# Routing the first half of the tokens earlier in a fused attention and mixture-of-experts kernel

## The reference

```python
x = L0_attn_x
h = _layernorm(x, axis=-1) * (1 + ca) + sa
x = x + ga * _L0_attn_ref(h, WQ, WK, WV, WO)      # causal attention, 16 heads of 8 channels
h = _layernorm(x, axis=-1) * (1 + cb) + sb
x = x + gb * _L0_ffn_ref(h, ...)                  # shared expert + routed experts

# _L0_ffn_ref: E = 64 experts in 8 groups; 4 groups kept, K = 6 experts for each token
shared = silu(x @ sg_w.T) * (x @ su_w.T) @ sd_w.T
scores = sigmoid(x @ gate_w.T) + gate_bias
...                                               # keep the best 4 groups, then the best 6 scores
comb = weights of the 6 chosen experts, normalised
h = silu(einsum('th,eih->eti', x, eg_w)) * einsum('th,eih->eti', x, eu_w)
routed = einsum('eti,ehi,te->th', h, ed_w, comb)
```

## Time and profile before

| | us |
|---|---|
| median of 3 runs | 1053.04 |
| lowest and highest | 1044.67, 1057.72 |
| the profiled execution, device time | 1046.67 |
| its span, first to last instruction | 1045.0 |
| PE busy in it | 869.2 |
| DVE busy | 724.9 |
| ACT busy | 565.3 |
| POOL busy | 253.7 |
| mean granted clock of TensorE, share of full | 0.912 |

### The profile page before, as it was taken

One profiled execution on the slowest core, in us unless ns is written; L12 is line 12 of the kernel. 1 busy time (PEld: TensorE's weight loads), 2 busy tenths in 40 slices (PEclk: granted clock), 3 DMA queues, 4 the chain that ended last, 5 costly groups with the idle time before them and its releaser, 6 DMA issues. The chain is left out here.

```text
span 1045.0 us, 13432 instructions
## 1 busy us (share of the span) xinstructions
PE 869.2 (83%) x4333; PEld 448.6 (43%) x4333; DVE 724.9 (69%) x1323; ACT 565.3 (54%) x888; POOL 253.7 (24%) x348
## 2 busy tenths in 40 slices
PE   6899999999885439998996006789999999998998
PEld 3553443444222219887886002333433443343433
DVE  4879888888476616655663234679988988997575
ACT  4324666666762105554553003649768877875743
POOL 1011222222115777714751771000000000000000
PEclk9899999999986579999998557879999999998999
DMA  3732565542012126746772112000000010000001
GB/s 88 236 79 45 190 198 172 160 144 70 23 53 93 51 87 216 229 158 200 225 222 92 52 51 73 0 0 9 2 23 11 7 46 1 0 1 0 1 0 41
DMA packets 51054, 87.48 MB, mean 84 GB/s; under 512 B 11202, under 2 KB 22832, under 8 KB 49200
## 3 DMA queue, kind: packets, MB, share of 16 engines
q1 hardware_dynamic: 36716, 58.56, 18.8%
q10 hardware_dynamic: 8128, 15.47, 4.0%
q0 software_dynamic: 6144, 12.60, 3.9%
HBM read 43.28 MB, written 40.89 MB: 81 GB/s over the span
## 5 line engine op out<-in xcount | busy, mean ns | idle before, releaser
L1066 ACT ACTIVATE pt<-psum 128x1024 f32<-128x1024 f32 (+1 forms) x192 | 149.9, 814 | 111.5 <-PE psum L808 111.1
L1218 DVE TENSOR_REDUCE part_max<-psum 128x1 f32<-128x512 f32 (+3 forms) x304 | 184.3, 658 | 31.6 <-PE psum L790 19.1
L786 PE MATMUL psum<-ka,qa 72*128 72x512 bf16 (+3 forms) x384 | 113.7, 337 | 5.4 <-DVE part_max L1218 2.0
L746 POOL DMA_INDIRECT part<-slot_y,slot_row x96 | 92.9, 968 | 86.5 <-DMA slot_y<-pt 57.8
L735 POOL DMA_INDIRECT slot_x<-va,slot_row x96 | 96.3, 1004 | 36.4 <-issue 29.0
L725 POOL TENSOR_SCALAR_AFFINE_SELECT pt<-pt 128x256 f32<-128x256 f32 x128 | 52.3, 410 | 215.4 <-ACT pt L1066 214.8
L808 PE MATMUL psum<-qa,ka 75*128 75x512 bf16 (+3 forms) x384 | 94.5, 328 | 3.0 <-ACT pt L1066 1.4
L824 PE MATMUL psum<-pt,va_g 128*32 128x512 f32 (+3 forms) x768 | 82.7, 503 | 0.5 <-POOL pt L725 0.3
L1426 DVE TENSOR_TENSOR moe_hid<-moe_silu,psum 128x256 f32<-128x256 f32 x56 | 23.4, 418 | 84.6 <-ACT moe_silu L1186 78.8
L110 ACT ACTIVATE ln_sq<-psum 128x512 f32<-128x512 f32 x44 | 26.1, 594 | 98.4 <-PE psum L93 98.3
L786 PEld LDWEIGHTS psum<-ka,qa 72*128 72x128 bf16 x384 | 37.1, 98 | 79.4 <-DVE part_max L1218 60.0
(11 more groups left out here) (316 smaller groups left out, 1650.3 us busy)
## 6 DMA issues: line engine op xcount, KB each, us to landing
slot_x<-zero ACTq DMA_DIRECT2D x8, 1792.0 KB, 7.0
pt<-slot_x SPq DMA_DIRECT2D x56, 256.0 KB, 3.4
slot_y<-pt SPq DMA_DIRECT2D x56, 256.0 KB, 2.0
qa<-in_moe_gu SPq DMA_DIRECT2D x4, 1024.0 KB, 6.3
qa<-rows_q SPq DMA_DIRECT2D x21, 192.0 KB
ka<-rows_k SPq DMA_DIRECT2D x21, 192.0 KB
wt_c<-in_channel_w SPq DMA_DIRECT2D x4, 576.0 KB, 4.2
o_den<-acc SPq DMA_DIRECT2D x32, 64.0 KB, 2.1
```

What stands on the lines that cost most here:

```text
L746: pool.indirect_dma_start(out=yg[:, n % 4, j, :], out_offset=None, in_=ys_d[b], in_offset=bass.IndirectOffsetOnAxis(ap=row[:, n, j:j + 1], ...
L786: mm = pe.matmul(bank[:, nk * h:nk * (h + 1)], qa[0:ROWS, g % RING, h0 + h, chunk(i, P)], ka[0:ROWS, g % RING, h0 + h, k0:k0 + nk], start= ...
L1066: act.activation(pt[:, u % 4, :, 0:n], score_bank[u % 2][:, :, 0:n], ACT.Exp, scale=SCALE)\
L1218: dve.tensor_reduce(part_max[:, h0:h0 + heads, slot], bank_of("fill", f)[:, 0:heads * nk].rearrange("p (h n) -> p h n", h=heads), AX_X, AL ...
```

## The change

The whole routing of batch 0 moves from group 7 and behind it into groups 3 to 6. A table, `STEP_AT`, gives each step of pieces 0 and 1 a unit, counted from EARLY = 72, the first unit of group 3; each step takes a place in the rotation of the three banks 4, 5 and 7 instead of a bank of its own, so the item three places on waits for its reader. DVE's and ACT's parts stand at the same units or a few later. `positions` is cut in parts (`counts`, `ranks`; `tile_ends`, `slot_keys`, `slot_rows`). For pieces 0 and 1 ACT copies the centred values to `G.h`, so that their bank comes free before `modulated` reads them. Scatters of batch 0 are issued one for each unit of `SCATTER_AT`: units 158 to 167 and 176 to 183, 18 in all; the other 30 follow the last mask. Behind attention, PE and DVE start with piece 2 at once.

```diff
+    EARLY = NU * 3
+    STEP_AT = {("project", 0): EARLY + 18, ("centre", 0): EARLY + 22, ("variance", 0): EARLY + 26, ("logits", 0): EARLY + 31,
+               ("turn_h", 0): EARLY + 34, ("project", 1): EARLY + 50, ("centre", 1): EARLY + 54, ("variance", 1): EARLY + 58,
+               ("logits", 1): EARLY + 63, ("turn_h", 1): EARLY + 66, ("count", 0): EARLY + 81, ("rank", 0): EARLY + 82,
+               ("experts", 0): EARLY + 88}
...
-        ITEMS += [("fill", f) for f in BACK[unit]]
+        ITEMS += [("fill", f) for f in BACK[unit]] + [item for item, at in STEP_AT.items() if at == unit]
+    SCATTER_AT = [u for u in range(EARLY + 86, NU * NG) if u < NU * LAST or 8 <= u - NU * LAST < 16]
...
+            if was == "project":
+                pe.wait_ge(x_new, k + 1)
+            if was == "centre":
+                pe.wait_ge(ln.squared, n0 + k + 1)
+                pe.wait_ge(centre_kept, k + 1)
...
-        centre_bank = [G.bank[4], G.bank[7], G.bank[4], G.bank[6]]
+        centre_bank = [bank_of("centre", 0), bank_of("centre", 1), G.bank[4], G.bank[6]]
...
+                        if NU * g + u in SCATTER_AT:
+                            scatter(0, SCATTER_AT.index(NU * g + u))
+                for k in range(len(SCATTER_AT), INDEXED):
+                    scatter(0, k)
+                for k in range(INDEXED):
+                    scatter(1, k)
...
                 def after_attention():
 
-                    positions(0)
+                    pe.wait_ge(v_in, NG)
                     turn_h(2)
-                    turn_experts(0)
                     project(3)
...
+                    if c < 2:
+                        act.copy(G.h[:, chunk(c)], centre_bank[c][:, :]).then_inc(centre_kept, 1)
...
+                def first_batch(unit):
+
+                    for c in range(2):
+                        if unit == STEP_AT["project", c] - 1:
+                            normalise(c)
+                        if unit == STEP_AT["project", c]:
+                            add_attention(c)
+                        if unit == STEP_AT["variance", c] + 1:
+                            modulated(c)
+                        if unit == STEP_AT["logits", c] + 1:
+                            route_scores(c)
+                        if unit == STEP_AT["logits", c] + 6:
+                            route_groups(c)
+                        if unit == STEP_AT["logits", c] + 10:
+                            route_mask(c)
+                        if unit == STEP_AT["logits", c] + 13:
+                            route_top(c)
+                        if unit == STEP_AT["logits", c] + 16:
+                            route_comb(c)
+                    if unit == STEP_AT["count", 0]:
+                        tile_ends(0)
+                    if unit == STEP_AT["rank", 0]:
+                        slot_keys(0)
+                    if unit == SCATTER_AT[0] - 2:
+                        slot_rows(0)
+                    if unit == STEP_AT["experts", 0] - 1:
+                        experts_of_tiles(0)
+                    if unit == STEP_AT["experts", 0]:
+                        keep_experts(0)
```

185 lines of the change are left out of this document (93 added, 92 removed).

## The result

Timed side by side, the changed kernel has a median of 1055.15 us (1043.85 to 1064.81, 20 runs) and the kernel before 1047.45 us (1041.62 to 1059.72, 20 runs): a ratio of 1.0056, with a 95% interval of 1.0029 to 1.0083. (The ratio is that of the mean times of the executions that lie within 1.5% of the fastest of their kernel, so it differs from that of the medians.) I had forecast a gain of 1% (10.7 us, 1040 us). The change costs about 6 us instead. That is less than 2%, and inside my range of 1025 to 1056, but on the other side of no change.

What follows compares the result with a forecast made beforehand. Attention was taken as PE-bound, DVE close behind, then POOL's 48 scatters decide. Attention's end moves 9.2 + 11.2 + 3.0 - 3.1 - 10.0 = +10.3 us, the tail -21.0: -10.7 from 1050.5, forecast 1040 us, range 1025 to 1056.

Steps and rivals of the forecast that it cites:

- E to the routed rows: From the last weighted-value matmul's end (E) to PE starting routed rows: 53.0 us instead of 72.2, shared expert deciding, not scatters.
- The 1.8 us on top: At the start of routed rows: PE, coming straight from matmuls, avoids the lower clock, 1.8 us less.
- PE's work in groups 3 to 6: Groups 3 to 6: moved projections, layer norm, logits, transposes, counts and ranks add 9.2 us, with no idle time hiding them.
- group 6's own gain: Group 6: 3.1 us less, from 31.7 to 28.6, as projections 0 and 1 and their pause leave its end.
- DVE's bunching: Groups 3 to 6: moved DVE steps fit in total but their bunching makes PE stand 11.2 us, bounds 3 and 19.2.
- masks: Units 160 to 167: POOL's masks queue behind scatters and delay weighted-value matmuls, 3.0 us more, bounds 0 and 5.
- rival C: In attention, stalls behind DVE's steps halve PE's clock, 3.1 us each; ten make it 1061 us or more; chance 0.07.
- the term of 10 us: Group 7: 10 us less, bounds 8 and 13, without batch 0's PE work, the 2.65 us pause and half clock.
- Rival B: Groups 3 to 6: DVE becomes the bound, routing costs 19.2 instead of 11.2, masks 5; 1050 us; chance 0.12.
- Rival A: Groups 3 to 6: the banks absorb DVE, stalls 3 us instead of 11.2, masks 0; 1029 us; chance 0.19.
- Rival D: Batch 0's slot rows are late, all 48 scatters fall behind the last mask; 1049 us; chance 0.04.
- clock windows under 1.00 in groups 3 to 6 (C): Sign in the new profile's groups 3 to 6 that the forecast is wrong and rival C holds.

Runs made afterwards that it cites:

- the order experiment: Kernel before with one edit: DVE normalises and adds piece 2 ahead of piece 1's scores instead of behind them; measured 0.9961 of the time before (0.9921 to 1.0001).

## Why the prediction was wrong, step by step

**E to the routed rows: right.** Forecast 53.0 us, measured 51.7. The rows wait no longer for a scatter but stand right behind the shared expert, as forecast:

```profile
397.72 1.13 PE L938 MATMUL psum<-o_den,shared_w 128*128 128x512 f32 x2 [0.85 <-DVE o_den L1477]
399.85 1.94 PE L945 MATMUL psum<-ident,pt 128*128 128x128 f32 x8 [1.00 <-issue]
```

POOL starts its 30 remaining scatters at 347.13, E - 1.1. The 1.8 us on top, which I gave PE for coming out of matmuls, did not appear: it came out of the shared expert at a full clock and the first eight transposes still took 1.94 us, as long as after the 16 us pause before. Four of the other kernels have the same 1.00 us of "issue" there and take 1.06 or 1.07 us, and the stretch behind the rows is 653.3 to 654.1 us in them, about 1 us less than before. But it is also 653.6 us in the kernel with the other order in group 7, which stands 18.34 us before it, so these traces don't tell whether any of the term exists. Why the clock had fallen just there in the changed kernel (399.8 to 403.2 us) stays open.

**PE's work in groups 3 to 6, 9.2 us: about right.** The kernel without early routing arithmetic has 9.1 us over 4 x 28.7, where 7.7 was forecast for its share (9.2 less 1.5). The other 1.4 us are then for the bank places and DVE's first 5.5 us of normalising and modulating, together. (By groups 3 to 5 alone it is 2.5 us, and group 6's own gain is then 3.9 us and not 3.1; the two errors nearly cancel.)

**DVE's bunching, 11.2 us (bounds 3 and 19.2), and masks, 3.0 (0 to 5): the stalls were right, their price was not.** Together I put them at 14.2 us of PE standing still. PE stands 10.4 us more than in the kernel without them. But it also works 15.2 us longer on the same matmuls, which no term had. (15.2 + 1.4 - 3.8 is 12.8 of the 13.1 us by which groups 3 to 6 exceed the forecast.) This is the step that failed: the sum put the clock's loss in groups 3 to 6 at nothing. The reason given stands in the prediction under rival C, "Against: single stalls should be 1 to 2 us, and groups 1 to 6 have a full clock with short waits". The stalls were 1 to 2 us, exactly as said, and the clock fell at 1.41 us. My evidence was of the wrong kind. The kernel before has waits of 0.8 us at most for maxima, all of them weight loads', and PE idle for next to nothing in group 4. It has a single pause between 1 and 2 us in groups 3 to 6, at the end of group 6:

```profile
277.25 1.13 PE L840 MATMUL psum<-o_den,wo_t 128*128 128x512 f32 x2 [1.49 <-DVE o_den L1252]
```

The clock stayed full there, and it fell within the pause of 2.65 us. So the record before had one such pause for and one against, and the prediction names only the second. One pause without a fall says little in any case: in the changed kernel three pauses of 1 to 2 us in groups 4 to 6 went without one and three had one, and the prediction set more than ten of DVE's steps among the maxima.

The Trainium skill, TensorE: Matmul & The Clock Gate (A second HAM failure mode), says of a kernel that cycles PSUM banks that short idles between groups of matmuls make the clock swing between its two levels and cost throughput. I had weighed this against group 4's clock of 1.00 and set it aside. The changed kernel agrees with the Trainium skill: 0.96, 0.77 and 0.90 in groups 4 to 6. Group 4 before had been no test, since PE never stood there.

**Rival C's price** was 3.1 us a fall, from one stretch of 6.7 us. The stretches in the changed kernel are 10.2, 20.5 and 6.8 us, so two falls cost what I had given five. "Four such falls cancel the gain" was too mild: three did, with the stalls. (The rival's "ten make it 2% slower, 1061 us or more" is a slip too: by its own price ten falls give 1050.5 - 10.7 + 31, 1071 us. And the lower bound of 3 us for the bunching is given without a sum; the working beside it, 2.8 a piece and 2.4, makes 8.0.)

**What the masks cost.** With ten scatters instead of eighteen, 2.3 + 2.1 us come back in groups 6 and 7 of the lumpy kernel and 3.3 + 0.9 in the one with parts; the timed ratios differ by 0.8% and 0.5%, 8 and 5 us. So the term of 3.0 (0 to 5) was about 4 us by the traces, the fall at 317.9 included, and 5 to 8 by the timed executions; the intervals of the second pair overlap. I had reckoned that POOL falls behind by 4 to 5 us and that 2 are forgiven. The direction was right. The block by DVE's instructions I had set aside on an average. That was too quick: at 238.30 one mask takes 0.89 us and not 0.41, beside the piece's `normalise` (a `TENSOR_TENSOR` from 238.25 to 238.93). But such masks are rare, and in the row of masks and scatters DVE had nothing to do from 312 to 318 us. What I missed is that I took the number of early scatters as given and did not ask how many are needed. By my own figures the shared expert ends at E + 53.0 and the rows trail the last scatter by 4.1 us, which leaves room for 38 scatters behind the last mask, not 30.

**Group 6's own gain and group 7.** Group 7 was to fall to 27.3 us and is 30.2; its first 6.8 us are at half clock. In the kernel with parts and ten scatters, which has no such stretch, it is 27.5, so the term of 10 us was right for a full clock. But the order experiment shows that 4.2 of it do not belong to the change at all.

**Rival B** (DVE busy throughout, 1050 us) comes near in time and has the wrong reason: DVE is busy 33.5 of 37.5 us in group 4, but 31.6 of 43.6 in group 5, the longest. **Rival A** fell with the stalls. **Rival D** (early scatters late) fell: all eighteen stand before the last mask. My list of what would show it wrong had the right sign in it, "clock windows under 1.00 in groups 3 to 6 (C)", so the failure is in the 0.07 that I gave it.

How the term splits is settled only roughly. Stalls and clock are not independent, since PE at half speed waits less for DVE (group 5 idles 1.8 us at 0.77); the 15.2 and 10.4 us are what these two traces have. Other executions will have had other falls, as the pauses of 1.97 and 1.04 us show. That they do so on average is borne out by the timed ratios of the kernels with parts and of the one with dummies, not by single stretches. What decides whether a given pause brings a fall stays open.

## What to carry to other kernels

Where PE is the bound and another engine empties its rotating banks, the extra work that this engine can take is not only a matter of its idle time but of the lumps it comes in: cut the work into small parts before moving it, and look at the longest waits, not only at the total. Price pauses of PE with the half clock that may follow, and several short ones close together as well as a single long one. It's a chance that you price, so ask many executions and not one trace. And don't take a full clock over a stretch with hardly a pause for evidence that it bears them. And when work is moved ahead to relieve an end, move only as much as brings it level with the next bound; the rest disturbs the place where it lands.

## What the runs showed of the hardware

- The clock fell to half in or shortly behind single pauses (1.41 us before 232.20, 1.04 before 267.30, 2.00 before 316.76), and in two kernels behind three pauses of 0.40, 0.67 and 0.52 us within 4 us. It stayed there for 3.4 to 20.5 us in groups 3 to 6. The pauses of 1.97 and 1.04 us each had a fall in one execution and none in another of the same instructions up to there.
- Dummy matmuls, four at a time (about 1.1 us) in 19 units, went with a clock of 1.00 over 114 us and paid for themselves: about 18 us more of PE busy, 5.6 us less in sum.
- An indirect DMA of POOL takes 0.97 us and 0.30 of "issue" behind another one, and 0.98 and 0.17 behind a mask; a pair of mask and scatter takes 1.60 us.
- POOL's masks in groups 4 to 6 take 423 ns on average beside the moved DVE steps, against 408 in the kernel before; most take 408 as before, but the one at 238.30 takes 892, beside a DVE instruction of 0.68 us with two inputs.
- The stretch ahead of group 3 varies by up to 8 us between executions, more than most edits here move, so single spans of this kernel are no measure of an edit.
